# A fused attention, state-space and expert kernel: the context's normalisation moved wholly to VectorE, in two passes

## The reference

```
xn = layernorm(ctx, ln1_w, ln1_b);   ln = layernorm(norm(x), ln2_w, ln2_b)
q = ln @ Wq;   k, v = split(concat(xn, ln) @ Wkv)          # 16 heads of 64
x = x + softmax(q k^T / 8) v @ Wo                          # per batch
layernorm(x, w, b) = (x - mean) * rsqrt(var + 1e-5) * w + b
```

## Time and profile before

| | us |
|---|---|
| median of 3 runs (lowest, highest) | 808.18 (807.22, 808.63) |
| the profiled execution, its own time | 806.97 |
| its span on the core | 805.2 |
| mean granted PE clock | 0.966 of full |

### The profile page before, as it was taken

The page is one execution under the profiler, slowest core; times in us unless marked ns, Lnnn a source line. Parts: engine busy times, 40 slices in busy tenths (PEclk is TensorE's granted clock), DMA queues, the critical chain, the costliest instruction groups (busy, mean ns, idle before and its releaser), DMA issues.

```text
span 805.2 us, 14296 instructions
## 1 busy us (share of the span) xinstructions
PE 733.7 (91%) x5387; PEld 675.1 (84%) x5387; DVE 514.3 (64%) x1098; ACT 409.4 (51%) x1086; POOL 419.5 (52%) x373
## 2 busy tenths in 40 slices
PE   4949999999999999999899999999999768899996
PEld 3549999999999899999899899998999757448895
DVE  5326557557565677797958668887688769860102
ACT  2523544555344566555666466454766426634341
POOL 3904402701350179667836996587478889960000
PEclk9989999999999999999999999999999975899999
DMA  8461010011001100220012003100011114902710
GB/s 313 182 214 15 1 60 24 2 59 24 1 2 59 50 8 9 73 50 15 9 59 53 18 9 91 25 20 1 15 28 24 20 27 130 335 0 105 253 62 29
DMA packets 49481, 49.86 MB, mean 62 GB/s; under 512 B 18484, under 2 KB 44288, under 8 KB 48256
## 3 DMA queue, kind: packets, MB, share of 16 engines
q1 hardware_dynamic: 49408, 48.90, 19.6%
HBM read 44.10 MB, written 4.79 MB: 61 GB/s over the span
## 4 chain that ended last, share of the span: by engine, by line
PE 52%; POOL 20%; DVE 13%; issue 9%; ACT 3%; DMA 2%; SPq 1%; POOLq 0%; DVEq 0%; ACTq 0%
PE psum L1607 14%; PE psum L1640 13%; PE psum L1623 4%; POOL work L616 4%; POOL y_sum L629 4%; PE psum L2027 4%; POOL work L623 3%; PE psum L2017 3%; DVE work L930 2%; PE psum L1580 2%; PE psum L1697 1%; POOL ctx_nat L578 1%; PE psum L1669 1%; POOL ctx_nat L577 1%; POOL kvn_lo L592 1%
## 5 line engine op out<-in xcount | busy, mean ns | idle before, releaser
L1282 ACT ACTIVATE pt_hi<-psum 128x512 fp32r<-128x512 f32 (+1 forms) x192 | 87.1, 489 | 214.0 <-PE psum L1623 160.1
L1640 PE MATMUL psum<-kvn_hi,pt_hi 128*128 128x256 f32 x512 | 150.5, 294 | 0.8 <-DVE pt_hi L850 0.8
L1640 PE MATMUL psum<-kvn_hi,pt_lo 128*128 128x256 f32 x512 | 145.0, 283 | 0.0
L1640 PE MATMUL psum<-kvn_lo,pt_hi 128*128 128x256 f32 x512 | 144.8, 283 | 0.0
L993 DVE TENSOR_REDUCE rowmax<-psum 128x1 f32<-128x728 f32 x64 | 58.5, 914 | 74.4 <-PE psum L1607 74.1
L623 POOL TENSOR_TENSOR work<-work,bc 128x512 f32<-128x512 f32 x48 | 65.8, 1370 | 65.0 <-DVE work L930 65.0
L1640 PEld LDWEIGHTS psum<-kvn_hi,pt_hi 128*128 128x128 f32 x512 | 98.0, 191 | 1.1 <-DVE pt_hi L850 1.0
L1607 PE MATMUL psum<-kvt_hi,qk_hi 128*128 128x364 f32 (+1 forms) x384 | 91.7, 348 | 7.4 <-ACT prob L1405 4.2
L1640 PEld LDWEIGHTS psum<-kvn_lo,pt_hi 128*128 128x128 f32 x512 | 98.1, 192 | 0.1
L1640 PEld LDWEIGHTS psum<-kvn_hi,pt_lo 128*128 128x128 f32 x512 | 97.8, 191 | 0.0
L853 DVE TENSOR_TENSOR pt_lo<-psum,pt_hi 128x512 fp32r<-128x512 f32 x128 | 81.9, 681 | 8.7 <-ACT pt_hi L1282 8.7
(11 more groups left out here) (237 smaller groups left out, 1551.2 us busy)
## 6 DMA issues: line engine op xcount, KB each, us to landing
w<-in_L_ffn_W_dram SPq DMA_DIRECT2D x16, 1024.0 KB, 8.2
ctx_nat<-in_ctx_dram SPq DMA_DIRECT2D x8, 1024.0 KB, 5.0
bc<-dbc_keep SPq DMA_DIRECT2D x48, 128.0 KB, 4.5
q_keep<-q_t SPq DMA_DIRECT2D x1, 2048.0 KB, 8.4
q_cur<-q_keep SPq DMA_DIRECT2D x14, 128.0 KB, 3.1
wk_nat<-in_L_xattn_Wkv_dram SPq DMA_DIRECT2D x1, 1024.0 KB, 6.0
wq_sb<-in_L_xattn_Wq_dram SPq DMA_DIRECT2D x1, 1024.0 KB, 12.0
wv<-in_L_xattn_Wkv_dram SPq DMA_DIRECT2D x1, 1024.0 KB, 14.1
```

The source lines that it names most:

```text
L1282: act.activation(pt_hi[u][:, t0:t1, :], where[:, 0:(t1 - t0) * P].rearrange("p (t m) -> p t m", m=P), ACT.Copy)\
L1640: pe.matmul(PV, w[u][:, j, :], x_[slot][:, j, :], start=(j == 0 and w is pt_hi and x_ is kvn_hi), stop=False)
```

## The change

POOL makes the latents' halves before it prepares batch 0. SP stores them first, waits for them, reads back the latents' rows, and goes on with the other stores. `ctx_affine` is gone. DVE normalises each context in two passes of 8 instructions with two tensor inputs each: `ctx_centre` computes (x - mean) * ln1_w, at hp 2, and `ctx_scale` computes that * rstd + ln1_b, at hp 3. Each instruction of the second pass waits for its own row block of the first. For batch 0 both passes run in the prologue.

```diff
 # SP
+            sp.wait_ge(s_xhl, 2)
+            sp.dma_start(x_keep[:, 0], x_hi[:].bitcast(F32)).then_inc(st_x, 16)
+            sp.dma_start(x_keep[:, 1], x_lo[:].bitcast(F32)).then_inc(st_x, 16)
             sp.wait_ge(s_pevac, 2)
             sp.dma_start(latt_keep[:, 0], latt_hi[:].bitcast(F32)).then_inc(st_keep, 16)
+            sp.wait_ge(st_x, 32)
+            for b in range(2):
+                load_latents(b)
             sp.wait_ge(s_plo, 1)
...
             sp.dma_start(q_keep, q_t[:]).then_inc(st_keep, 16)
-            sp.wait_ge(s_xhl, 2)
...
 # POOL
-                link(pool.tensor_tensor(crstd[:], cvar[:], mhalf[:], ALU.pow))
-                link(pool.tensor_tensor(cnm[:], cmv[:, :, 0], crstd[:], ALU.mult))
-                pool.tensor_scalar(cshift[:], cnm[:], -1.0, 0.0, ALU.mult, ALU.add).then_inc(s_csh, 1)
-            def ctx_affine(b, q):
...
+                pool.tensor_tensor(crstd[:], cvar[:], mhalf[:], ALU.pow).then_inc(s_csh, 1)
...
+            latent_parts()
             ctx_norm(0)
-            for q in range(4):
-                ctx_affine(0, q)
             ctx_high(0, 0)
             ctx_low(0, 0)
-            latent_parts()
...
-                    if 3 <= hp < 7:
-                        ctx_affine(b + 1, hp - 3)
 # DVE
+            def ctx_centre(b):
+                if b == 0:
+                    dve.wait_ge(ld_vec, 32)
+                dve.wait_ge(s_cmv, b + 1)
+                for j in range(SJ):
+                    dve.scalar_tensor_tensor(out=ctx_nat[:, j, :], in0=ctx_nat[:, j, :], scalar=cmv[:, j, 0:1],
+                                             in1=ln1wb[:, 0, :], op0=ALU.subtract, op1=ALU.mult).then_inc(s_cz, 1)
             def ctx_scale(b):
                 dve.wait_ge(s_csh, b + 1)
                 for j in range(SJ):
-                    last = dve.tensor_scalar(ctx_nat[:, j, :], ctx_nat[:, j, :], crstd[:, j:j + 1],
-                                             cshift[:, j:j + 1], ALU.mult, ALU.add)
-                last.then_inc(s_cz, 1)
+                    dve.wait_ge(s_cz, SJ * b + j + 1)
+                    dve.scalar_tensor_tensor(out=ctx_nat[:, j, :], in0=ctx_nat[:, j, :], scalar=crstd[:, j:j + 1],
+                                             in1=ln1wb[:, 1, :], op0=ALU.mult, op1=ALU.add).then_inc(s_cn, 1)
...
+            ctx_centre(0)
             ctx_scale(0)
...
                 if more and hp == 2:
+                    ctx_centre(b + 1)
+                if more and hp == 3:
                     ctx_scale(b + 1)
```

More of the change, by code:

```diff
@@ L143, in perceiver_kernel @@
         crstd = sb(att, "crstd", [P, SJ])
-        cnm = sb(att, "cnm", [P, SJ])
-        cshift = sb(att, "cshift", [P, SJ])
         mhalf = sb(att, "mhalf", [P, SJ])
@@ L564, in ctx_norm @@
                 link(pool.tensor_scalar(cvar[:], cmv[:, :, 1], 1.0, EPS, ALU.mult, ALU.add))
-                link(pool.tensor_tensor(crstd[:], cvar[:], mhalf[:], ALU.pow))
-                link(pool.tensor_tensor(cnm[:], cmv[:, :, 0], crstd[:], ALU.mult))
-                pool.tensor_scalar(cshift[:], cnm[:], -1.0, 0.0, ALU.mult, ALU.add).then_inc(s_csh, 1)
-            def ctx_affine(b, q):
[L571 to L578, removed]
+                pool.tensor_tensor(crstd[:], cvar[:], mhalf[:], ALU.pow).then_inc(s_csh, 1)
             def ctx_high(b, slot):
-                pool.wait_ge(s_cn, 4 * b + 4)
+                pool.wait_ge(s_cn, SJ * (b + 1))
                 if b >= 2:
@@ L1584, in misc @@
                     if k == 0:
-                        pe.wait_ge(s_cn, 4 * b + 2 * h + 2)
+                        pe.wait_ge(s_cn, SJ * b + 4 * h + 4)
                     for j in range(4):
```

## The result

The changed kernel takes **824.0 us** (median of 4 runs, 822.2 to 824.9) where the kernel before took 807.9 beside it: a ratio of 1.019, 95% interval 1.017 to 1.021. The profiled execution took 822.22 us, its span is 820.5. The forecast was 812.4 with a range from 803.5 to 819. The direction was right, the size was not: +16.1 where +4.2 was forecast.

The account below looks back on a forecast made before the run. PE, busy 91% of the span, was taken as the bound, so only its waits and low clock count. Terms -5.5 - 1.5 + 10.7 - 2.9 + 3.4 = +4.2 us gave a median of 812.4 us, range 803.5 to 819.

Parts of the forecast that it names:

- Start with its clock: Batch 0: second head pair's reduction starts earlier, -5.5 us, and the half-clock spell can go, -1.5 us.
- Batches 0 to 2: Second pass at hp 3 in early batches: rowmax 1.4 us late, hidden by PE's own work, cost 0.
- Batches 3 to 6, hp 2 to 4, without the clock: Second pass, blocked by POOL, delays the rowmax: +1.8, +2.6, +3.0, +2.9; with the first pass's 0.4, +10.7 us.
- Clock behind the four waits: After new PE waits at part C, batches 3 to 6, the clock falls: +3.4 us, bounds 0 and +6.8.
- POOL's rest: Without POOL's context quarters, DVE scans at hp 6 are unblocked and PE waits shrink: -2.9 us, bounds 0 and -5.0.
- the lateness of the rowmax: Rowmax behind the second pass in batches 3 to 6 starts 4.1, 4.6, 6.1 and 4.3 us late.
- So 2.36 us of lateness cost nothing.: Hp 4 logits: 5.74 us from rowmax to logits, only 3.38 needed, so 2.36 us of rowmax lateness is free.
- the forecast went by `conv` and the turned tokens: Batches 4 and 6, hp 4: turned tokens at 375.4 for 372.83 (+2.6) and 530.6 for 527.66 (+2.9).
- I take two: Of four new waits at part C, two count as clock falls of about 1.7 us each: +3.4 us.
- The first pass: DVE's pass at hp 2, 0.4 us longer than before, hidden by PE except in batch 6: +0.4 us.
- One bound of the prediction: Second pass never blocked by POOL: lateness 2.2, 1.4, 3.6 and 0 in batches 3 to 6, costing +0.4 us.
- the hidden second pass: Rival, 15%: less POOL work and 2.36 us of room hide the second pass, -9.1 us, giving 799 us.

Follow-up runs that it names:

- e2: The changed kernel with the second pass one head pair later, at the end of hp 4 instead of hp 3: 804.2 us, ratio 0.995.
- e4: The changed kernel with dummy PE transposes filling the wait at part C of hp 4 in batches 3 to 6: 818.4 us, ratio 1.013.
- e3: The changed kernel with one-input statistics instructions replacing the second pass, scale and shift left out of the result: 802.5 us, ratio 0.993.
- e7: The changed kernel with both DVE passes but the start's old order on POOL and SP: 830.4 us, ratio 1.026.
- e1: The kernel before with only the start's new order on POOL and SP, context normalisation as before: 802.7 us, ratio 0.993.

## Why the prediction was wrong, step by step

Measured from the row maxima of the two profiled executions (before and after the change):

| Term | forecast | measured |
|---|---|---|
| Start with its clock | -7.0 | -7.5 |
| Batches 0 to 2 | 0 | +2.0 |
| Batches 3 to 6, hp 2 to 4, without the clock | +10.7 | +14.5 |
| Clock behind the four waits | +3.4 | +8.0 |
| Batches 3 to 6, hp 5 to 7 (POOL's rest) | -2.9 | -2.0 |
| Batch 7 | 0 | +1.6 |
| From the last rowmax to the end | 0 | -1.4 |
| Sum | +4.2 | +15.2 |

**Right:** the start, and the lateness of the rowmax: 4.1, 4.6, 6.1 and 4.3 forecast for batches 3 to 6; 4.4, 4.9, 6.7 and 4.2 found as the difference of the cumulated row maxima. So the price of a pass of two-input instructions was right, 3.1 forecast and 3.25 measured alone, 5.8 forecast and 5.5 to 6.35 beside three of POOL.

**The step that failed** is "So 2.36 us of lateness cost nothing." The 3.38 us that it subtracted came from the second pair of batch 0, where PE has neither `head_out` nor key products between part C and the next logits. At hp 4 it has both, and `head_out` waits for a copy that DVE makes after the rowmax; e2 shows 3.38 again at an odd hp, the changed kernel 4.95 at hp 4. The room is 0.79. That is 0.65 in each of batches 0 to 2, and it explains batch 3 (4.41 - 0.79 = 3.6; measured 3.6 without the clock, forecast 1.8).

Batch 5 cost near 5.2 without the clock (7.5 for hp 2 to 4, less 0.6 of e4 and the 1.7 of its windows; forecast 3.0). Here the kernel before is another case, with DVE waiting for POOL:

```profile
451.87 2.24 DVE L930 TENSOR_TENSOR_SCAN work<-dec,work 128x512 f32<-128x512 f32 x1 [3.04 <-POOL work L616]
...
455.07 0.91 DVE L993 TENSOR_REDUCE rowmax<-psum 128x1 f32<-128x728 f32 x1
```

One rowmax followed the other after 455.07 - 445.46 = 9.61 us. At full clock and without this wait e3 needs 8.23, so 1.4 us was free at this step, and 6.7 - 1.4 = 5.3.

In batches 4 and 6 the forecast went by `conv` and the turned tokens, and the number was right: 2.9 and 2.8 measured for 2.6 and 3.3. That is in part luck. PE's path through `head_out` and the key products, which the forecast left out, ends last there too, at full clock 0.2 us behind `conv` (e4), in the changed kernel without a wait for `conv` at all.

**The second failed step** is "I take two" of four clock falls at 1.7 us. All four came and cost 2.0 each on average. In each a second wait, of 0.7 to 0.9 us for `y_t`, follows on the first; whether it has a part in the fall no run shows. That the range ended at 819 has the same cause: its upper end counted dearer terms one at a time, not two errors with one sign.

**POOL's rest** gave two thirds of what was taken: batches 4 and 6 gave 1.1 each, but 3 and 5 gave 0.9 and 0.5 at hp 6 or 5 and lost 0.8 each at hp 7.

**The first pass** cost 0.6, 0.7, 0.6 and -0.3 in batches 3 to 6 where 0.4 was forecast in batch 6 alone (in the table within hp 2 to 4).

**Batch 7.** Its +1.6 is no effect of the passes: e7 has the same ones and shows nothing there. It stands with the fall of the clock that the last section tells of.

One bound of the prediction was misread without effect: never blocked, the pass of batch 6 would end at 519.6 + 3.1 = 522.7, so its rowmax, at 521.27 before, would be 1.4 late and not 0.

Of the rivals, the hidden second pass (799) was ruled out by the waits; its number is near e2 and e3, that is with the pass at another step or without its second input. By the Trainium skill (VectorE: DVE Perf Modes, "Why `tensor_tensor` can't do 2×_2P or 4×") eight two-input instructions would be 1.1 us dearer than eight with one input, an estimate from its rate. The trace shows 3.25 against 2.67 us, 0.6, and the measurement decides.

## What to carry to other kernels

Read the room in front of a step at that same step, with everything that the waiting engine issues between the late event and the work it must be in time for: here two items that only some steps have made 2.36 us into 0.79. Before adding work to an engine that another one follows closely, try the neighbouring steps: with the second pass one place later the two cost 1.5 us by the medians instead of 21. And price a stall of TensorE like the four here (2.1 to 4.6 us) twice: once as a wait and once, here for about 2 us, at the lower clock. The next section shows that a fall need not follow.

## What was not expected of the hardware

**The same short wait is followed by a fall of the clock in one execution and by none in another.** In batch 7 PE waits 1.28 us (L1758) at 627 and then runs at 0.59 from 630 to 634; in the kernel before the wait is 1.26 us and the next window (616 to 620) is at 1.00. At the start e1 and e2 have the same wait of 3.50 us for `prob` at 47; the windows behind it, of e1 and then of e2:

```profile
48.00:52.00 4.00, 3.73 (x26) 3.47 (x24) 1.10 (x2) 0.67 (x2) 0.00 (x0) 1.00 1.04 306
```

```profile
48.00:52.00 4.00, 4.00 (x18) 3.92 (x17) 0.15 (x1) 0.00 (x0) 0.00 (x0) 0.57 0.93 232
```

The two executions differ by 3.0 us in the time from the first to the third rowmax, two thirds of what the runs of e1 scatter by (4.6). What decides it no run shows. It bears on e2 as well: of the 3.9 us that e2's execution is behind e1's at the first rowmax of batch 7, 2.4 were there at the third rowmax of batch 0, before any pass of the middle, so the second pass at hp 4 may cost less than the medians say.

The length of the spell differs, too: behind the same wait at hp 4 of batch 3 the clock was down for some 4 us in the changed kernel (0.54 and 0.60 in two windows of 2 us) and for some 7 in e7 (0.94, 0.50, 0.50, 0.50 and 0.86).
